# The wide attention of the first layer: values in dense pairs of heads, each head's product in one half of TensorE's rows and columns

## The reference

```python
q  = layernorm(x) @ Wq                     # (64, 64, 1024): 16 heads of 64
kv = ctx @ Wkv ; k, v = split(kv)          # (64, 64, 1024) each
p  = softmax(q_h @ k_h.T + mask)           # for each sequence and head: 64 x 64
o  = p @ v_h                               # 64 x 64
x  = x + tanh(attn_gate) * (concat_h(o) @ Wo)
x  = x + tanh(ff_gate) * (gelu(layernorm(x) @ W1) @ W2)
```

## Time and profile before

| | |
|---|---|
| time before, median of 3 runs | 3127.86 us (3121.6 to 3136.8) |
| the profiled execution's own time | 3139.09 us |
| span of its instructions | 3137.3 us, 50209 instructions |
| busy PE | 2890.7 us (92%) |
| busy PE weight loads | 1672.5 us (53%) |
| busy DVE, ACT, POOL | 1641.2, 1576.1, 1057.8 us |
| mean granted TensorE clock | 0.966 |

### The profile page before, as it was taken

How to read it: one execution, slowest core, us unless ns; L and a number is a source line. 1 busy time by engine, 2 the same in 40 slices (tenths; PEclk the granted TensorE clock), 3 DMA queues, 4 the chain that set the end, 5 groups by cost and what they waited for, 6 DMA issues and landing times.

```text
span 3137.3 us, 50209 instructions
## 1 busy us (share of the span) xinstructions
PE 2890.7 (92%) x16725; PEld 1672.5 (53%) x16725; DVE 1641.2 (52%) x3803; ACT 1576.1 (50%) x6978; POOL 1057.8 (34%) x998
## 2 busy tenths in 40 slices
PE   6999999989999999898999998988999999998898
PEld 3556455555565545555555554545555556455454
DVE  3435367565443536656544454665645444466664
ACT  2437455745343835464533383656544357275462
POOL 1014154452111415445211241543521133255352
PEclk9999999999998999999999999999999999999999
DMA  5010110102100011010210101111021000110111
GB/s 177 1 31 1 37 39 21 45 25 61 58 1 31 1 41 35 25 42 24 62 58 1 31 2 41 35 27 50 25 62 48 8 24 2 45 51 15 41 35 38
DMA packets 170981, 109.36 MB, mean 35 GB/s; under 512 B 31650, under 2 KB 168292, under 8 KB 170596
## 3 DMA queue, kind: packets, MB, share of 16 engines
q1 hardware_dynamic: 166272, 105.82, 11.9%
q10 hardware_dynamic: 4452, 0.29, 0.1%
HBM read 101.87 MB, written 4.19 MB: 34 GB/s over the span
## 4 chain that ended last, share of the span: by engine, by line
PE 65%; DVE 15%; ACT 13%; issue 4%; POOL 2%; ACTq 1%; DVEq 0%
PE proj L952 10%; ACT Ebuf L1368 10%; PE acc L1290 5%; PE pt_bank L1018 4%; PE proj L1190 4%; PE acc L1199 4%; PE acc L1178 3%; PE proj L1171 3%; PE scores L1007 3%; PE o_bank L1034 3%; PE proj L957 3%; PE scores L997 2%; PE proj L1224 2%; PE o_bank L1052 2%; PE proj L1141 2%
## 5 line engine op out<-in xcount | busy, mean ns | idle before, releaser
L1368 ACT ACTIVATE Ebuf<-scores,minus_max 128x64 f32<-128x64 f32 x2592 | 776.0, 353 | 226.9 <-DVE minus_max L1565 225.9
L1750 POOL TENSOR_TENSOR Ebuf<-Ebuf,row_rcp 128x512 f32<-128x512 f32 (+1 forms) x328 | 344.8, 1052 | 1014.2 <-DVE row_rcp L1572 1008.5
L1368 ACT ACTIVATION_READ_ACCUMULATOR Ebuf<-scores,minus_max 128x1 f32 x2592 | 620.6, 246 | 0.0
L1565 DVE TENSOR_REDUCE minus_max<-scores 128x8 f32<-128x512 f32 (+1 forms) x328 | 222.3, 680 | 295.4 <-PE scores L984 114.6
L1377 ACT ACTIVATE PT<-pt_bank 128x512 f32<-128x512 f32 (+1 forms) x328 | 205.0, 625 | 163.4 <-PE pt_bank L1018 161.7
L1018 PE MATMUL pt_bank<-ident,Ebuf 128*128 128x128 f32 x1296 | 213.1, 288 | 6.7 <-POOL Ebuf L1750 5.8
L952 PE MATMUL proj<-xs_a,w_ring 128*128 128x512 f32 (+1 forms) x384 | 192.9, 626 | 5.2 <-DVE arena_a L1720 5.2
L1572 DVE RECIPROCAL row_rcp<-row_sum 128x8 f32<-128x8 f32 (+1 forms) x328 | 65.6, 200 | 242.7 <-ACT Ebuf L1368 240.7
L952 PE MATMUL proj<-xs_b,w_ring 128*128 128x512 f32 (+1 forms) x384 | 186.9, 610 | 4.3 <-DVE xs_b L1640 4.1
L1018 PEld LDWEIGHTS pt_bank<-ident,Ebuf 128*128 128x128 f32 x1296 | 145.5, 145 | 81.2 <-issue 60.3
L1796 POOL TENSOR_TENSOR arena_b<-arena_b,masks_b 128x384 f32<-128x384 f32 (+1 forms) x48 | 67.7, 1411 | 222.2 <-DVE arena_b L1720 222.2
(11 more groups left out here) (317 smaller groups left out, 6228.3 us busy)
## 6 DMA issues: line engine op xcount, KB each, us to landing
w_ring<-in_L_W SPq DMA_DIRECT2D x64, 256.0 KB, 3.1
w_ring<-in_L_l_gate SPq DMA_DIRECT2D x80, 128.0 KB, 2.2
w_ring<-in_L_l_up SPq DMA_DIRECT2D x80, 128.0 KB, 2.3
w_ring<-in_L_l_down SPq DMA_DIRECT2D x80, 128.0 KB, 2.2
w_ring<-in_L_v_gate SPq DMA_DIRECT2D x80, 128.0 KB, 2.4
w_ring<-in_L_v_up SPq DMA_DIRECT2D x80, 128.0 KB, 2.4
w_ring<-in_L_v_down SPq DMA_DIRECT2D x80, 128.0 KB, 2.4
arena_a<-in_x SPq DMA_DIRECT2D x4, 512.0 KB
```

The costliest lines, as they stand in the source:

```text
L1368: last = A(Ebuf[:, u % 3, cell], score_bank[u % 2][:, cell], ACT.Exp, bias=minus_max[:, u % 3, c:c + 1], accum_out=row_sum[:, u % 3, c:c + 1])
L1565: V.reduce_max(minus_max[:, u % 3, 0:g], cells(score_bank[u % 2][:, 0:g * S]), AX_X, negate=True).then_inc(maxed, 1)
L1750: G_.tensor_tensor(v, v, row_rcp[:, n % 3, 0:g].unsqueeze(2).broadcast_to([P, g, S]), ALU.mult).then_inc(probs_ready, 1)
```

## The change

The values are no longer kept block-diagonally. `l1_v` holds for each pair of steps (j and its odd or even partner) all 8 sequences with head 0 of a step in partitions 0 to 63 and head 1 in partitions 64 to 127, dense, and it has two buffers of such pairs in the same space.

- `l1v` of step j now makes the values of both steps of the pair, for half of the sequences: 8 matmuls of 128 rows by 64 columns that stream 128 columns, head e into the e-th half of the partitions. DVE takes them out in one copy of 128x512.
- `pv` runs two matmuls for each sequence, one a head, of 64 rows by 64 columns, with head e in rows 64e to 64e+63 and in columns 64e to 64e+63: 16 matmuls or 32 passes a step.
- `zero_v` is gone. DVE waits for `l0pv` itself ahead of the first `l1v`.
- `pv` of step j waits for both `l1v` of its pair. The copy of `l1v` from step 4 on waits for the last `pv` of the pair two before.
- Four entries of the planner's tables change with it: `pv` of l1 on PE from 1.85 to 1.3, `l1v` on PE from 1.0 to 1.05 and on DVE from 1.7 to 0.7, and `zero_v` is taken out.

```diff
-        return chain(("PE", {"l1": 1.85, "self": 0.4, "cross": 0.55}[kind]), ("DVE", {"l1": 0.7, "self": 0.45, "cross": 0.3}[kind]))
+        return chain(("PE", {"l1": 1.3, "self": 0.4, "cross": 0.55}[kind]), ("DVE", {"l1": 0.7, "self": 0.45, "cross": 0.3}[kind]))
...
-        st.l1_vbd = part(A_QK, 2, G, P)
+        st.l1_v = part(A_QK, 2, G, 2, S)
...
-                    pe.wait_ge(*l1_v_ready[s].at(turn, j + 1))
+                    pe.wait_ge(*l1_v_ready[s].at(turn, j // 2 * 2 + 2))
                     for n in range(G):
-                        last = mm(o_bank[:, n * S:(n + 1) * S], st.l1_vbd[:, j % 2, n, :], probs[:, n * S:(n + 1) * S],
-                                  start=True, stop=True)
+                        for e in range(2):
+                            rows = slice(64 * e, 64 * e + 64)
+                            last = mm(o_bank[rows, n * S:(n + 1) * S], st.l1_v[rows, j // 2 % 2, n, j % 2, :],
+                                      probs[rows, n * S:(n + 1) * S], start=True, stop=True)
...
-                        for p in range(PAIRS):
-                            last = mm(b[:, p * P:(p + 1) * P], st.ctxT[:, p * P:(p + 1) * P],
-                                      w_kv[:, L1_INNER + j * P:L1_INNER + (j + 1) * P], start=True, stop=True)
+                        w_v = w_kv[:, L1_INNER + j // 2 * 2 * P:L1_INNER + (j // 2 + 1) * 2 * P].rearrange("p (a e d) -> p a e d", a=2, e=2)
+                        for c in range(G // 2):
+                            n = j % 2 * (G // 2) + c
+                            for e in range(2):
+                                last = mm(b[64 * e:64 * e + 64, c * P:(c + 1) * P], st.ctxT[:, n * S:(n + 1) * S], w_v[:, :, e, :],
+                                          start=True, stop=True)
...
                     if j == 0:
-                        dve.wait_ge(*vbd_zeroed[s].at(turn, 1))
-                    if j >= 2:
-                        dve.wait_ge(pv_done, PV[s, turn, ("l1", j - 2)] + 1)
+                        dve.wait_ge(*filled(("l0pv", s, turn, 1)))
+                    if j >= 4:
+                        dve.wait_ge(pv_done, PV[s, turn, ("l1", j // 2 * 2 - 3)] + 1)
                     dve.wait_ge(*filled(token))
-                    for r in range(2):
-                        for e in range(2):
-                            src = b[64 * r:64 * r + 64, :].rearrange("p (c e d) -> p c e d", c=PAIRS, e=2)[:, :, e, :]
-                            last = V.tensor_copy(st.l1_vbd[64 * e:64 * e + 64, j % 2, r:r + 2 * PAIRS - 1:2, 64 * e:64 * e + 64], src)
-                    last.then_inc(l1_v_ready[s].sem, 1)
+                    some = slice(j % 2 * (G // 2), (j % 2 + 1) * (G // 2))
+                    V.tensor_copy(st.l1_v[:, j // 2 % 2, some, :, :], b[:, :].rearrange("p (n a d) -> p n a d", n=G // 2, a=2)
+                                  ).then_inc(l1_v_ready[s].sem, 1)
...
-                if step == "zero_v":
-                    pool.wait_ge(*filled(("l0pv", s, turn, 1)))
-                    G_.memset(st.arena[:, A_QK:A_QK + 2048], 0.0).then_inc(vbd_zeroed[s].sem, 1)
```

More of the change, by code:

```diff
@@ L63, in l0_stage @@
              (4.8, "memN", 0), (5.7, "memN", 1), (7.0, "scores", ("l0", 0)), (9.5, "prob", ("l0", 0)),
-             (12.0, "trans", ("l0", 0)), (14.0, "l0pv", 0), (15.0, "l0pv", 1), (15.5, "zero_v"), (16.0, "zero_k"), (17.0, "gate", 0),
+             (12.0, "trans", ("l0", 0)), (14.0, "l0pv", 0), (15.0, "l0pv", 1), (16.0, "zero_k"), (17.0, "gate", 0),
              (20.5, "gate", 1), (22.0, "fuse", 0), (24.0, "fuse", 1)]
@@ L235, in parts @@
         "mem": (("PE", 0.95), ("ACT", 0.6)), "memN": (("PE", 1.0), ("DVE", 0.7)), "l0pv": (("PE", 1.0), ("ACT", 0.6)),
-        "zero_v": (("POOL", 1.8),), "zero_k": (("POOL", 1.8),), "zero_s": (("POOL", 1.8),), "gate": (("PE", 3.75), ("ACT", 0.7)),
-        "fuse": (("DVE", 1.6),), "mean": (("PE", 1.87), ("DVE", 1.5)), "l1k": (("PE", 0.95), ("ACT", 1.2)), "l1v": (("PE", 1.0), ("DVE", 1.7)),
+        "zero_k": (("POOL", 1.8),), "zero_s": (("POOL", 1.8),), "gate": (("PE", 3.75), ("ACT", 0.7)),
+        "fuse": (("DVE", 1.6),), "mean": (("PE", 1.87), ("DVE", 1.5)), "l1k": (("PE", 0.95), ("ACT", 1.2)), "l1v": (("PE", 1.05), ("DVE", 0.7)),
         "l1q": (("PE", 1.87), ("ACT", 0.6)), "wo": (("PE", 1.87),), "res1": (("DVE", 1.5),), "res2": (("DVE", 1.5),), "res3": (("DVE", 1.4),),
@@ L273, in follows @@
             if key[0] == "l1":
-                return of(None, ("trans", key), ("l1v", key[1])) + of("PE", ("wo", key[1] - 2))
+                return of(None, ("trans", key), ("l1v", key[1] | 1)) + of("PE", ("wo", key[1] - 2))
             return of(None, ("trans", key), ("v", key[1], 1) if key[0] == "self" else ("values", key[1], key[2] // 2))
@@ L301, in follows @@
         return of(None, ("silu", *where)) + of("PE", ("down", n, last - 2))
-    return {"l0pv": of(None, ("trans", ("l0", 0)), ("memN", 0), ("memN", 1)), "zero_v": of("PE", ("l0pv", 1)), "zero_k": of("PE", ("l0pv", 1)),
+    return {"l0pv": of(None, ("trans", ("l0", 0)), ("memN", 0), ("memN", 1)), "zero_k": of("PE", ("l0pv", 1)),
             "gate": of(None, ("l0pv", 0), ("l0pv", 1)), "fuse": of(None, ("gate", 0), ("gate", 1)),
@@ L306, in follows @@
             "l1k": of(None, ("ctx",), ("zero_k",)) + of("PE", ("scores", ("l1", last - 2))) if last is not None and last > 1 else of(None, ("ctx",), ("zero_k",)),
-            "l1v": of(None, ("zero_v",)) + (of("PE", ("pv", ("l1", last - 2))) if last is not None and last > 1 else []),
+            "l1v": of("PE", ("l0pv", 1)) + (of("PE", ("pv", ("l1", last // 2 * 2 - 3))) if last is not None and last > 3 else []),
             "l1q": of(None, ("spread", 1, 0), ("l1k", last)), "wo": of(None, ("pv", ("l1", last))), "res1": of(None, ("wo", JT - 1)),
@@ L723, in xattn_kernel @@
     gate_scaled, fused = pair("gate_scaled", 2), pair("fused", 2)
-    kbd_zeroed, vbd_zeroed, v_zeroed = pair("kbd_zeroed", 1), pair("vbd_zeroed", 1), pair("v_zeroed", 1)
+    kbd_zeroed, v_zeroed = pair("kbd_zeroed", 1), pair("v_zeroed", 1)
     centred = pair("centred", 4)
```

## The result

The changed kernel takes 3075.55 us (median of 4 runs, 3065.9 to 3081.4) against 3129.59 us of before. The ratio is 0.9829 with a 95% interval of 0.9809 to 0.9850: 54 us or 1.7% less, where 41 us or 1.3% was forecast. The profiled execution took 3077.1 us.

The account below looks back on a forecast made before the run. The prediction took PE to set the time in L1. Its terms, -40 (pv) + 6 (l1v on PE) - 4 (l1v on DVE) - 3 (pauses) = -41 us, took 3127.9 us to 3087 us, range 3064 to 3116 us.

Parts of the forecast that it names:

- the likeliest case: Whole kernel: the forecast itself, 3087 us, with 30 to 57 us gained, 3071 to 3098 us; chance 0.65.
- pv on PE: pv in L1: 32 passes take 1.13 us in place of 1.83 us, 0.70 us a step, 44.8 us over 64 steps.
- Nine tenths of it count: PE in L1: of the 44.8 us that pv's passes gain, 40 us shorten the span.
- rival B: L1: the softmax sets the step in one of two halves, half of pv's gain goes: 3105 us; chance 0.17.
- l1v on PE: l1v in L1: 16 passes take 1.03 us, a loss of 0.08 to 0.10 us a step, 6 us in all.
- l1v on DVE: DVE in L1: one copy of 0.69 us replaces four totalling 1.68 us; shorter PE waits gain 4 us, bounds 0 and 10.
- a wait above 1 us for this line: Sign for DVE's l1v copy, line 1656: no PE wait for it above 1 us.
- DVE's busy time: Sign on DVE: with 64 copies of 0.69 us at line 1656, busy time falls by some 64 us.
- Pauses: Pausing matmuls on PE: 228 in place of 253, 25 fewer are 5.5 us; half taken, a gain of 3 us.
- The stretches: Sign by stretch: a's L1 shorter by 4 to 5 us, b's by 5 to 6 us, all others the same.
- rival D: PE's granted clock: the mean falls from 0.966 to about 0.948, ending within 0.5% or slower; chance 0.04.
- Rival C: pv in L1: row halves cannot write one bank together, pv takes 2.26 us, +26 us, 3154 us; chance 0.09.

Follow-up runs that it names:

- heads_in_turn: The changed kernel with pv's loop over the two heads outside the loop over the sequences, 16 passes in one half and then 16 in the other: 3121.0 us.
- columns_only: The kernel before with pv as 32 passes of all 128 rows by 64 columns, the zeros multiplied too: 3090.9 us, ratio 0.9866.
- pv_only: The kernel before with one edit, pv as 32 passes of 64 rows by 64 columns; order, pauses, store and zeros stay: 3098.2 us, ratio 0.9886.
- old_costs: The changed kernel planned with the costs of before for pv (1.85) and l1v (1.0 and 1.7); only order and pauses differ: 3094.0 us, ratio 0.9879.
- four_copies: The changed kernel with DVE's single copy of each l1v cut in four of 64 partitions, as before: 3092.1 us, ratio 0.9900.
- no_pauses: The changed kernel without any of its 228 pausing matmuls: 3120.8 us, ratio 0.9959.

## Why the prediction was right, point by point

The direction, the range (3064 to 3116 us) and the likeliest case held; the point, 3087 us, was 11 us too slow against 3075.6 us, or 13 us in the difference. The parts, however, did not come as summed, and that the point is so near is luck in part.

- *pv on PE*, 0.70 us a step or 44.8 us: right. 0.75 us a step was measured, 48 us in all, and line 972 was the right row to take it from. That two halves must run by turns is shown by heads_in_turn; that column halves are enough, by columns_only. The prediction had looked at the row halves (line 1115's seam) for what the column halves give. The modelled length of a pass is 0.218 us, as forecast.
- *Nine tenths of it count*: mis-sized. In the old order 24 of the 48 us count (pv_only), since the earlier trace rows show no waits only as long as `pv` itself fills the time of the softmax. This was rival B, and it is right for that kernel. In the new order nearly all counts (heads_in_turn: 43 of 46.7 us). The likely reason is that `wo` stands ahead of the transposes in more of the steps, 35 of the 42 in which the trace tells, against 26 of 42 in old_costs and 28 of 39 before: the transposes wait 5.6 us in all for POOL, against 9.9 us in old_costs and 11.6 us in pv_only. No run moves `wo` alone. A list of waits tells what is late now, not how late the next one is.
- *l1v on PE*, a loss of 6 us: the length was right, 1.03 us. With the waits that follow it, the groups of `l1v` grew from 70.7 to 82.8 us, 12 us.
- *l1v on DVE*, 4 us: four_copies gives 7.9 us. The term was mis-sized by half, within its bounds of 0 to 10 us. New waits for the copy stand at the start of the feed-forward (8.7 us in three waits), where the `l1v` of the next stream is queued on DVE behind a norm. The prediction held a wait above 1 us for this line to be unlikely. The one of them in turn 1 also cost clock: over the 2.5 us after it the granted clock was 0.50, and the 8 passes behind it took 5.0 us; in old_costs the same 8 passes follow PE's work closely and took 3.67 us:

```profile
926.57 5.16 PE L1197 MATMUL proj<-xs_a,w_ring 128*128 128x512 f32 x8 [2.89 <-DVE arena_b L1656]
```

- *DVE's busy time*, 64 us less: the copies of the values lost that (107.3 to 43.5 us), but DVE as a whole only 49 us. Its other operations, the same in number, took 15 us longer. No run shows why.
- *Pauses*, 3 us: their groups lost 9.8 us in the profiled execution, but no_pauses shows that they cannot be counted alone, as they hold the clock.
- *Planner's order*: the prediction gave it no term. old_costs puts 7 us on it at equal clock.
- *The stretches*: forecast were 4 to 5 us less in a's L1, 5 to 6 us less in b's, and the others the same; turn 1 shows 2 us more, 17 us less, and 8.6 us less in the stretch behind. The prediction itself had named this as the sign that the planner or the clock, which the sum leaves alone, had acted. By its own test the sum was not the whole account.
- The sum at equal clock, 40.3 us, is the forecast's 41 us, by errors that cancel. Shares of single parts depend on what is changed first. Taken first, `pv` gives 23.7 us (pv_only) and all the rest 16.6 us; the copy's 7.9 us (four_copies) and the costs' 7.3 us (old_costs) nearly make up this rest. Taken last, `pv` gives 43.2 us, and all the rest without it is 2.9 us slower than before (heads_in_turn). So the other parts pay by letting the faster `pv` count.
- *The clock*, rival D: it was there, with the other sign. (0.9762 - 0.9695) x 2250 us = 15 us are the part that the forecast lacks. It was treated as a risk of loss alone, although L1 of b had a mean clock of 0.93, and so something to win. Its price was too high as well: the 0.018 of clock that it sets against 57 us are 3.1 us for each thousandth, where the executions show 2.25 us. Why the clock is higher is not settled. pv_only, with the order and the pauses of before, already has 0.9742, heads_in_turn, with `pv` as long as before, 0.9740, and old_costs, with as many pauses as the changed kernel but for six, 0.9712. No one part accounts for it.
- *Rival C*, the halves take turns: refuted in one bank as well (pv_only). heads_in_turn is what it would have looked like, without its further loss: 1.83 us a step and not 2.26 us.

## What to carry to other kernels

Where a matmul streams fewer columns than it loads as weights, cut the weights into column halves and issue the halves by turns, not one after the other. Here that held for three groups: `pv` (1.83 to 1.08 us), `l0pv` (3.3 to 1.94 us) and the sums (0.81 to 0.56 us). The store of the operands need not change for it. Then look at what the shortened group was hiding, and compare kernels at equal mean clock before any few microseconds are put down to a part.

## What was not expected of the hardware

- 16 passes that load 128 columns and 32 passes that load 64 columns, first all in one half and then all in the other, take the same 1.83 us; the 32 passes by turns take 1.08 us.
- With 128 weight columns a pass takes about the same time whatever it streams up to 128 columns: 0.10 us with 1 column (the sums, 0.81 us for 8), 0.114 us with 64, 0.111 us with 128.
- Times and mean clock of the same kernel lie on a line of 2.25 us a thousandth within 1.2 us. Nearly all of the scatter of before, 3110.6 to 3143.1 us, goes with the clock.
- The 228 pausing matmuls of the changed kernel hold the mean clock at 0.976; without them it is 0.948, at 45 us more.
- A change of the planner's costs alone moved the mean clock between 0.9622 and 0.9800.
